# Feature-major input, weights loaded whole and tiles assembled by GpSimd copies at the head of a mixed adapter, attention and MLP kernel

## The reference

```python
x = adapter(x, role, L0 weights)          # layer 0
x = attention_and_mlp(x, code, L1 weights) # layer 1
x = adapter(x, role, L2 weights)          # layer 2
x = adapter(x, role, L3 weights)          # layer 3

def adapter(x, role, Wd, bd, Wu, bu, gamma, beta):   # Wd 3x256x128, Wu 3x128x256
    u = gelu(x @ Wd[role] + bd[role]) @ Wu[role] + bu[role]
    return layernorm(x + u) * gamma[role] + beta[role]

def attention_and_mlp(x, code, ...):       # V = 256, H = 1024
    q, k, v = x @ Wq, x @ Wk, x @ Wv
    ao = softmax(q k^T / 16) v @ Wp + bp   # within each sequence
    cms = gelu(ao @ cW1 + cb1) @ cW2 + cb2 + one_hot(code)
    mod = gelu(concat(ao, cms) @ mW1 + mb1) @ mW2 + mb2
    return clip(x + cms + mod, 0, 1)
```

## Time and profile before

| | us |
|---|---|
| median of 3 runs (195.21 to 195.64) | 195.59 |
| the profiled execution's own time | 195.45 |
| its span, first to last instruction | 193.7 |

### The profile page before, as it was taken

How to read it: one execution, slowest core, us unless ns; L and a number is a source line. 1 busy time by engine, 2 the same in 40 slices (tenths; PEclk the granted TensorE clock), 3 DMA queues, 4 the chain that set the end, 5 groups by cost and what they waited for, 6 DMA issues and landing times.

```text
span 193.7 us, 3157 instructions
## 1 busy us (share of the span) xinstructions
PE 184.1 (95%) x1031; PEld 157.8 (81%) x1031; DVE 114.3 (59%) x283; ACT 80.8 (42%) x164; POOL 42.1 (22%) x72
## 2 busy tenths in 40 slices
PE   7979999999999999999999999999999999999980
PEld 7858787979888888778888888888888989999860
DVE  2986998799658608982193522041432136558983
ACT  0733764643798206672045544003445333222340
POOL 8474667100000006000140000000100013226431
PEclk9999999999999999999999999999999999999996
DMA  3778589993301130330000060000100003442122
GB/s 103 235 215 277 162 272 270 279 307 125 108 0 46 68 108 0 108 112 0 0 0 3 0 193 24 0 0 5 54 0 0 3 0 108 123 127 69 41 61 77
DMA packets 18874, 17.83 MB, mean 92 GB/s; under 512 B 2145, under 2 KB 17322, under 8 KB 18858
## 3 DMA queue, kind: packets, MB, share of 16 engines
q1 hardware_dynamic: 17008, 14.79, 24.8%
q0 software_dynamic: 928, 2.11, 4.1%
q10 hardware_dynamic: 922, 0.73, 1.2%
HBM read 16.58 MB, written 1.05 MB: 91 GB/s over the span
## 4 chain that ended last, share of the span: by engine, by line
PE 78%; DVE 11%; DMA 5%; issue 2%; ACT 1%; POOL 1%; ACTq 0%; DVEq 0%
PE bank L640 20%; PE bank L641 19%; PE bank L642 19%; PE bank L752 5%; PE bank L768 5%; DMA stage<-in_L_cond_Wq 2%; PE bank L745 2%; DMA x_tok<-in_x,from_row_i 2%; PE bank L821 2%; PE bank L808 2%; PE bank L778 1%; DVE yA L1331 1%; PE bank L747 1%; DVE yB L1350 1%; DVE cms_l L1433 1%
## 5 line engine op out<-in xcount | busy, mean ns | idle before, releaser
L1412 DVE TENSOR_TENSOR g_l<-g_full,g_h 128x512 fp32r<-128x512 f32 x32 | 21.8, 691 | 36.1 <-ACT g_h L1037 36.0
L1034 ACT ACTIVATE g_full<-bank,vecs 128x512 f32<-128x512 f32 x32 | 22.1, 691 | 43.4 <-PE bank L642 40.4
L1524 POOL TENSOR_TENSOR mvA<-mvA,power 128x1 f32<-128x1 f32 x16 | 9.4, 588 | 70.6 <-DVE mvA L1267 70.6
L1037 ACT ACTIVATE g_h<-bank,vecs 128x512 fp32r<-128x512 f32 x32 | 22.0, 687 | 0.0
L1551 POOL TENSOR_TENSOR x1T<-x1T,cms_full 128x512 f32<-128x512 f32 x4 | 6.0, 1498 | 57.2 <-DVE cms_full L1427 57.2
L640 PE MATMUL bank<-g_h,mw_h 128*128 128x256 f32 (+1 forms) x48 | 16.0, 334 | 0.0
L642 PE MATMUL bank<-g_h,mw_l 128*128 128x256 f32 (+1 forms) x48 | 15.3, 318 | 0.0
L641 PE MATMUL bank<-g_l,mw_h 128*128 128x256 f32 (+1 forms) x48 | 15.3, 318 | 0.0
L640 PE MATMUL bank<-ao_h,mw_h 128*128 128x512 f32 x32 | 13.2, 411 | 0.0
L640 PE MATMUL bank<-ao_h,cw_h 128*128 128x512 f32 x32 | 12.8, 400 | 0.1
L642 PE MATMUL bank<-ao_h,mw_l 128*128 128x512 f32 x32 | 12.5, 391 | 0.0
(11 more groups left out here) (265 smaller groups left out, 441.5 us busy)
## 6 DMA issues: line engine op xcount, KB each, us to landing
stage<-in_L_cond_mW SPq DMA_DIRECT2D x6, 512.0 KB, 3.3
stage<-in_L_cond_cW SPq DMA_DIRECT2D x4, 512.0 KB, 5.8
wdA<-in_L_cond_W_down SPq DMA_DIRECT2D x14, 128.0 KB, 3.8
wuA<-in_L_cond_W_up SPq DMA_DIRECT2D x14, 128.0 KB, 3.8
wdB<-in_L_cond_W_down SPq DMA_DIRECT2D x12, 128.0 KB, 3.3
wuB<-in_L_cond_W_up SPq DMA_DIRECT2D x12, 128.0 KB, 3.2
wd_last<-in_L_cond_W_down SPq DMA_DIRECT2D x4, 128.0 KB, 2.3
wu_last<-in_L_cond_W_up SPq DMA_DIRECT2D x4, 128.0 KB, 2.3
```

The lines of the kernel that those rows point to most:

```text
L1034: act.activation(g_full[n % 2][:, 0:width], bank[b][:, 0:width], ACT.Gelu, bias=bias)
L1037: act.activation(g[0][:, j, 0:width], bank[b][:, 0:width], ACT.Gelu, bias=bias).then_inc(g_high, 1)
L1412: dve.tensor_tensor(g[1][:, j, 0:width], g_full[n % 2][:, 0:width], g[0][:, j, 0:width].bitcast(F32), ALU.subtract).then_inc(g_ready, 1)
L1524: pool.tensor_tensor(mv[:, k, 2:3], mv[:, k, 1:2], power[:, :], ALU.pow).then_inc(done, 1)
```

## The change

The host now lays out the inputs: x feature-major ([128, 2, 1024]), the square matrices already transposed where they need to be, W_down and W_up of a role side by side (512 columns), the biases stacked once as rows and once as columns, and the role and code numbers together. In the kernel:

- x comes in whole with one DMA (`x_all`, 1 MB), and so do all three roles' weights of adapter 0 (`w_all`, 768 KB). POOL loads the row numbers of the sequences into registers and assembles each tile with four copies of 128 x (2 x 32) elements. No gather, no PE transposes of `load`, no ACT copy.
- The weights of the first four passes are copied by ACT out of `w_all` by a register (`first_weights`); of all later passes they are fetched with one DMA of 256 KB instead of two of 128 KB.
- `fold_transpose` and `vectors` are gone. `fold(0, *)` stands ahead of `order`; `fold(1, 0)` stands after `down(0, 3)` and `fold(1, 1)` after `up(0, 3)`; `fold_low(1)` after `turn(0, 3)`.
- `hot` of full tiles is a column with a stride of 0 as the matmul's operand. The row numbers of tokens, still needed for stores, are made by eight small DVE instructions after `hidden(0, 3)` (`rows`), and the four indirect DMAs of `token_tables` follow there.
- `late_biases` stands after `center(0, 5)`, its first copy is ACT's. Five DMAs of POOL and its memset of `bu_rows` are gone; DVE does that memset.
- The first piece of the MLP weights is asked for after pass 5 of layer 0 instead of at the start, ahead of the mixed passes.
- `warm` goes from 10 + 3 to 9 + 1 + 1.

The core of the diff:

```diff
 def plan():
     return [
-        ("warm", 10), ("fold_transpose", 0), ("fold_transpose", 1), ("warm", 3), ("order",), ("pick_vecs",),
-        ("fold_transpose", 2), ("spread",), ("fold", 0, 0), ("first_hot",), ("fold", 0, 1), ("fold_low", 0),
-        ("fold", 1, 0), ("chunk_vecs",), ("vectors",), ("sort_rest",), ("load", 0, 0), ("fold", 1, 1),
-        ("load", 0, 1), ("fold_low", 1), ("down", 0, 0), ("down", 0, 1), ("load", 0, 2), ("sort_codes",),
-        ("up", 0, 0), ("up", 0, 1), ("center", 0, 0), ("load", 0, 3), ("rest",), ("down", 0, 2), ("load", 0, 6),
-        ("down", 0, 3), ("center", 0, 1), ("up", 0, 2), ("late_biases",), ("turn", 0, 0), ("center", 0, 2),
+        ("warm", 9), ("spread",), ("fold", 0, 0), ("fold", 0, 1), ("order",), ("pick_vecs",), ("first_hot",),
+        ("load", 0, 0), ("first_weights", 0), ("warm", 1), ("chunk_vecs",), ("load", 0, 1), ("first_weights", 1), ("warm", 1),
+        ("fold_low", 0), ("sort_rest",), ("load", 0, 2), ("down", 0, 0), ("first_weights", 2), ("down", 0, 1),
+        ("load", 0, 3), ("first_weights", 3), ("up", 0, 0), ("up", 0, 1), ("center", 0, 0), ("rest",), ("down", 0, 2),
+        ("load", 0, 6), ("down", 0, 3), ("fold", 1, 0), ("center", 0, 1), ("up", 0, 2), ("turn", 0, 0), ("center", 0, 2),
+        ("up", 0, 3), ("load", 0, 7), ("seq_vecs",), ("fold", 1, 1), ("turn", 0, 1), ("center", 0, 3), ("load", 0, 4),
...
         @block.sync
-            sp.dma_start(roles_i[:, :], a["itok_B_1_2"].partition_broadcast(P)).then_inc(ids_in, 16)
+            sp.dma_start(ids[:, :], a["ids"]).then_inc(ids_in, 16)
+            sp.wait_ge(bu_zero, 1)
+            sp.dma_start(bu_rows[0:2 * R, :, :], a["b_up"]).then_inc(bu_in, 16)
+            sp.dma_start(x_all[:, :, :], a["x"]).then_inc(x_all_in, 16)
+            sp.dma_start(w_all[:, :, :], a["adapters"][0].rearrange("r p n -> p r n")).then_inc(w_all_in, 16)
+            for w in "vp":
+                sp.dma_start(wT[w][:, :, :], square_from(w)).then_inc(square_in[w], 16)
...
-            for n in range(PASSES):
+            for n in range(COPIED, PASSES):
+                if passes_of(0)[n] == (MESSY[0], FULL):
+                    piece(0)
...
         @block.tensor   (down)
-                pe.wait_ge(hot_ready, 1 if c < MESSY[0] else 2)
+                pe.wait_ge(hot_ready, 2 if c in MESSY else 1)
...
+                    hot = hot_col[:, full_column(c):full_column(c) + 1].to_broadcast([P, P])
...
         @block.scalar
+            for w in "qk":
+                act.dma_start(wT[w][:, :, :], square_from(w)).then_inc(square_in[w], 16)
+            act.dma_start(vec_rows[:, :], a["vec_rows"][0:PER_ROLE * R, :]).then_inc(vectors_in, 16)
+            act.dma_start(vecs[:, :], a["vecs"]).then_inc(vecs_in, 16)
...
+            def first_weights(n):
+                if n == 0:
+                    act.wait_ge(chunks_ready, 1)
...
+                    act.wait_ge(w_all_in, 16)
+                act.copy(wA[n][:, :], w_all[:, bass.ds(first_role[n], 1), :].rearrange("p r n -> p (r n)")).then_inc(wA_in[n], 16)
...
         @block.gpsimd
+            def load(layer, c):
+                if layer:
+                    return
+                if c == 0:
+                    pool.wait_ge(seats_ready, 1)
+                    load_seats(EARLY[0:1])
+                    pool.wait_ge(x_all_in, 16)
+                elif c == EARLY[1]:
+                    load_seats(EARLY[1:3])
+                elif c == EARLY[3]:
+                    load_seats(EARLY[3:])
+                elif c == MESSY[0]:
+                    pool.wait_ge(rest_seats_ready, 1)
+                    load_seats(MESSY)
+                for j in range(WB):
+                    ins = pool.tensor_copy(x0[place_of(0, c)][:, :, S * j:S * (j + 1)], x_all[:, :, bass.ds(seat_row[c, j], S)])
+                ins.then_inc(x0_ready, 1)
```

More of the change, by code:

```diff
@@ L128, in plan @@
+        ("down", 0, 6), ("down", 0, 7), ("turn", 0, 2), ("weights", 0, 0), ("up", 0, 6), ("up", 0, 7), ("turn", 0, 3),
+        ("fold_low", 1), ("center", 0, 6), ("split", 0, 0), ("load", 0, 5), ("down", 0, 4), ("center", 0, 7),
         ("turn", 0, 6), ("down", 0, 5), ("project", 0, 0), ("weights", 0, 1), ("turn", 0, 7), ("up", 0, 4),
         ("project", 0, 1), ("split", 1, 0), ("center", 0, 4), ("up", 0, 5), ("turn", 0, 4),
-        ("center", 0, 5), ("scores", 0), ("values", 0, 0), ("probs", 0), ("values", 0, 1), ("turn", 0, 5),
+        ("center", 0, 5), ("late_biases",), ("scores", 0), ("values", 0, 0), ("probs", 0), ("values", 0, 1), ("turn", 0, 5),
@@ L866, in outer @@
                             mm.then_inc(outer_ps, 1)
[L868 to L870 removed]
+            do = {"warm": keep_warm, "order": find_order, "rest": rest, "chunk_vecs": chunk_vectors, "seq_vecs": seq_vectors,
+                  "codes": codes_sorted, "fold": fold,
+                  "down": down, "up": up, "turn": turn, "values": values, "project": project, "scores": scores, "mix": mix,
                   "hidden": hidden, "outer": outer}
@@ L1505, in rest @@
-            def rest():
-                pool.wait_ge(rest_rows_ready, 1)
-                for c in (d for d in range(WIN) if d not in EARLY):
-                    gather(c)
-                pool.memset(probs_T[:, :, :], 0.0).then_inc(constants, 1)
-            def token_tables():
-                pool.wait_ge(token_roles_ready, 1)
+            iota(part_col2[:, :], [[0, 1]], P, 1).then_inc(constants, 1)
+            pool.memset(probs_T[:, :, :], 0.0).then_inc(constants, 1)
+            seat_row = {}
@@ new lines, in load_seats @@
+            def load_seats(tiles):
+                lo, n = row_column(tiles[0]), len(tiles)
+                _, values = nc.values_load_multi_w_load_instructions(
+                    seat_row_i[0:1, lo:lo + n, :].rearrange("p w j -> p (w j)"), engines=[mybir.EngineType.Pool],
+                    min_val=0, max_val=N - S,
+                    skip_runtime_bounds_check_because="a sum of one row number of 0 to 992 and zeros")
+                seat_row.update(zip([(c, j) for c in tiles for j in range(WB)], values))
```

401 lines of the change are left out of this document (160 added, 241 removed).

## The result

| | before | after |
|---|---|---|
| median us (lowest to highest) | 195.46 (195.21 to 195.64, 4 runs) | 199.37 (198.19 to 199.99, 4 runs) |
| profiled execution, us | 195.45 | 198.95 |
| its span, us | 193.7 | 197.0 |
| PE busy, us | 184.1 | 184.2 |

The ratio is 1.0184, 95% interval 1.0149 to 1.0219: 1.8% slower, where 192.5 (faster) was forecast. PE's busy time is the same although it has 998 matmuls instead of 1031, and some of these took twice their time; its idle time grew from 9.6 to 12.8 us.

A forecast was written before the change was run, and what follows sets the result against it. PE was taken as the bound from its first real pass to the tail. 195.45 - 3.6 (earlier `scores`) + 0.3 (`late_biases`) = 192.1, the median 0.14 above; with 0.3 for stalls, 192.5. Forecast 191.8 to 194.0, wider range 190.6 to 195.4.

The forecast's parts named there:

- Role numbers and order: In the head: roles arrive 1.0 us earlier, `order` at 7.5 behind the folds, row numbers copied by 7.9.
- Weights by ACT: In the head: 2.43 MB at 350 GB/s, `w_all` there at 10.6, first copied weights at 11.2.
- First passes: From `down(0,0)` to the fourth `down`: the latter starts at 14.65 instead of 19.47, 4.8 us earlier.
- From the fourth `down` to `scores`: 15.4 us before, net 1.2 added by folds less transposes; `scores` at 31.2 instead of 34.85, 3.6 us gained.
- Behind it: After `scores`: `late_biases` on DVE ahead of the first softmax step loses 0.3 us; the other items counted 0.
- tiles by POOL: Tile assembly in the head: 0.15 us a copy, 0.6 a tile; first tile at 9.5 us, fourth at 13.2.
- The first rival: POOL's tile copies cost 0.55 us each, fourth `down` only at 18.95; time 197.6, chance 0.10.
- decision point of 0.45 us a copy: POOL's tile copies: the price from about which the slow-POOL case, 197.6 us, decides.
- the sum: Whole kernel: 195.45 - 3.6 + 0.3 = 192.1, then 192.5 with 0.3 for stalls between engines.
- The rival of the clock: PE's clock falls back between 7.6 and 11.2 us, fourth `down` at 17.0; time 194.6, chance 0.12.
- The argument against it: Against a clock fall: before, PE was busy only 0.42 of 12 to 13 us, yet transposes after kept 0.11.

The follow-up runs named there:

- e4: e3 with the v, p and later adapter weights asked for only after `w_all` has landed; 193.43 us, ratio to before 0.9852.
- e1: The changed kernel plus eight matmuls of zeros in the head where PE was idle; 196.45 us, ratio to before 1.0031.
- e3: The changed kernel with the edits of both e1 and e2; 193.14 us, ratio to before 0.9869; on another occasion 193.73 us, 0.9925.
- e8: e3 with the tile of `down(0,5)` put back behind `split(0,0)` in POOL's list; 195.11 us, ratio to before 0.9964.
- e7: e3 plus 56 useless POOL copies of 128 x 64 during `hidden(1,*)` in the MLP; one execution, 193.98 us.
- e2: The changed kernel with POOL's assemblies of tiles 6, 7, 4 and 5 moved earlier in its list; 194.60 us, ratio to before 0.9874.
- e9: e3 with the first four passes' weights fetched by role, without `w_all` or ACT's copies; 193.55 us, ratio to before 0.9887.

## Why the prediction was wrong

The span forecast was 190.7 (193.7 less 3.0, in which 0.3 is set aside for stalls between engines), measured 197.0. By its own steps, in the order of the prediction:

1. *Role numbers and order*: right. `order` at 7.49 for 7.5, the row numbers ready at 8.11 for 7.9. POOL's first register load, 0.53 us for the 0.95 forecast, was hidden by the wait for x_all, which landed only after 9.0; the first tile was there at 10.0 instead of 9.5.
2. *Weights by ACT*: first copy at 11.58 for 10.6, so 1.0 us late. The step divided the bytes by a mean rate; e4 shows a tail of 2 us in which little moves before the request is complete. No row gave the 0.4 us for the receipt; in e4 0.5 us pass from 11.0, when the packets are through, to ACT's start at 11.47. In the experiments the copy varied from 10.94 to 11.99.
3. *First passes*: from that copy to the fourth `down` 4.05 us were forecast; with the clock up it is 4.6 (e1) and 4.9 (e3), and after it was 5.95. So 0.6 for hand-overs and 1.3 for the clock. Fourth `down` 17.53 for 14.65.
4. *From the fourth `down` to `scores`*: 16.6 forecast. The work was sized rightly: e3 has 16.4, folds included. After it was 20.2: 2.2 for POOL's late tiles (e1 has 18.6) and 1.6 for the second fall of the clock. Of the 2.2, 1.3 are the contention at the last tile (e8), which leaves 0.9 for tile 7's place in the list.
5. *Behind it*: `scores` to the end of the span was 158.85 and is 159.30, 0.45 for the 0.3 forecast.

Together 1.0 + 0.6 + 1.3 + 2.2 + 1.6 - 0.2 = 6.5 us at `scores` (31.2 forecast, 37.70 measured); with the 0.15 behind it and without the 0.3 set aside, that is the 6.3 us of the span. The largest part, 2.9, is the clock, and 2.2 are POOL's tiles.

Two steps of the prediction failed. The first is the one on tiles by POOL. It sized the copy and then asked only whether the fourth tile is there in time; the tiles 6, 7, 4 and 5 were given no place. Each stands in POOL's list behind a power that waits for DVE, so a tile can't come before DVE is ready for something else. And the copy's price was one price, where it has two: 0.18 us from one to the next alone, and the rest of DVE's instruction, up to 1.32 us, beside one that works on SBUF. The first rival named POOL as slow and had a single price too; its decision point of 0.45 us a copy was passed only by the last tile, with 0.6. The rule of the Trainium skill quoted there (SBUF — State Buffer, "Who interferes with whom"), that a DVE instruction with two SBUF inputs contends with a GpSimd instruction that reads SBUF, agrees with the 1.32 us of e7; the prediction let it raise a chance and gave it no time. The same section has copies and casts able to contend when they run in a 2-port mode, with the other engine blocked for the whole instruction, which fits the 0.69 and 0.78 us beside a rounding, though no run here shows the mode.

The second is that the sum left the matmuls at full clock: it put the fall of the clock in a rival and took nothing for it, where two falls cost 2.9 us.

The rival of the clock was right in kind, at a chance of 0.12. It priced one fall at about 2.4 us, where one cost 1.3 to 1.6, and did not see that a POOL wait opens a second gap. The argument against it was weak: a kernel that gets through a thin stretch once says little of one that is thinner. Rows 1 had a sign of it that the prediction passed over: in the last 8.7 us PE is busy 2.97 and the clock is 0.82 on the mean (it fell at 190.5, 2.5 us after the last matmul). The two losses did not add: e1 won 2.9 us and e2 4.8, but both edits together 6.2, since in many executions either edit alone kept the clock up.

With both taken away the kernel stands at 193.1 to 193.7, 0.6 to 1.2 us above the forecast of 192.5. So the gain of the change as a whole was there: by the two ratios (0.9869 and 0.9925 of 195.5) 2.6 and 1.5 us. What each part of it gave is shown only for the weights, by e9.

## What to carry to other kernels

When work moves to another engine, find a place for every piece of it in that engine's order, not only for the first: a piece behind an instruction that waits is as late as that wait. Price a GpSimd operation twice, alone and beside the VectorE instructions of the same time, where a copy may have to stand until the VectorE instruction is over, and put it where VectorE is idle or reads PSUM. Where an edit empties TensorE's head, fill it with matmuls of zeros in its idle time; here eight of them (e1) bought 2.9 us, and a mean clock per execution shows whether it worked in all of them.

## What the runs showed of the hardware

- A POOL copy of 128 x 64 took 0.23 us, with 0.18 from one start to the next, while DVE was idle, read PSUM or did small work. Beside a DVE instruction that works on SBUF alone it ended 0.09 to 0.10 us after that instruction, in all 36 copies longer than 0.30 us: 1.32 us at most beside a subtraction of 128 x 1024, 0.69 to 0.78 beside a rounding of 128 x 1024.
- The granted clock fell to 0.50 (1.2 GHz) twice in one execution, the first time after a thin stretch with 1.66 us without a matmul, the second after 1.5 us without one; the same gap left it at 1.00 in the profiles of e1 and e8. Each fall of 3.4 us cost 1.3 to 1.6 us. In e2 it stayed down from 11.5 to 21.8 us, and that execution took 4.4 us more than the median of the faster five.
- With 1 MB and 768 KB asked for together and nothing behind them (e4), the DMA share was 0.83 from 8 to 9 us and 0.11 to 0.28 from 9 to 11, and ACT got the second request only at 11.47.
- A stationary operand of stride 0 loaded as fast as a dense one: 0.19 us for each of 18 loads after and of 24 before.
- On POOL a load of 4, 8 and 12 registers took 0.53, 0.58 and 0.81 us (8.15, 9.50 and 10.99 in the changed kernel).
